# Spreading the inverse sums of an attention kernel: whole-array matmuls against row tiles of 32

## The reference

```
sc = where(causal, q k^T / 4, -inf), cut into key windows of 128
probs = e / sum(e)        with e = exp(sc - max), inside each window of 128 keys
attn  = softmax(probs)    over all 1024 keys; then attn @ v
```

## Time and profile before

| | |
|---|---|
| Three runs, median (lowest to highest) | 2868.73 us (2865.2 to 2870.33) |
| Profiled execution: span (no time of its own is given) | 2862.7 us |
| Mean granted clock of TensorE over the span | 0.967 of full speed |
| PE, DVE, ACT, POOL busy, share of the span | 90%, 76%, 63%, 21% |
| Last chain of work: PE, DVE, waiting for nothing shown, ACT | 49%, 29%, 15%, 4% |
| Of it, by line: L1152, L1075, L565, L516, L618, L580 | 11%, 7%, 7%, 6%, 5%, 3% |

### The profile page before, as it was taken

How to read it: one execution, slowest core, us unless ns; L and a number is a source line. 1 busy time by engine, 2 the same in 40 slices (tenths; PEclk the granted TensorE clock), 3 DMA queues, 4 the chain that set the end, 5 groups by cost and what they waited for, 6 DMA issues and landing times.

```text
span 2862.7 us, 58460 instructions
## 1 busy us (share of the span) xinstructions
PE 2562.9 (90%) x21797; PEld 1415.5 (49%) x21884; DVE 2179.6 (76%) x2854; ACT 1810.4 (63%) x2772; POOL 589.1 (21%) x518
## 2 busy tenths in 40 slices
PE   4799898999989999899989999899898999989877
PEld 2354464444544455444554445554464444644444
DVE  4687868788778877878778787787868888688755
ACT  2288844887358772677627886288843888358761
POOL 0012023120322104220132212212123120321004
PEclk8699999999999999999999999999999999999998
DMA  3412211231121220222202212022311131121000
GB/s 109 82 24 65 41 52 35 41 65 33 43 57 30 54 53 26 54 34 49 55 28 50 60 24 74 13 46 60 43 55 35 31 75 24 52 56 24 1 30 15
DMA packets 97791, 128.66 MB, mean 45 GB/s; under 512 B 21064, under 2 KB 58184, under 8 KB 97488
## 3 DMA queue, kind: packets, MB, share of 16 engines
q1 hardware_dynamic: 97488, 124.58, 20.4%
HBM read 90.94 MB, written 33.60 MB: 44 GB/s over the span
## 4 chain that ended last, share of the span: by engine, by line
PE 49%; DVE 29%; issue 15%; ACT 4%; POOL 1%; DMA 1%; DVEq 1%; SPq 0%; POOLq 0%; ACTq 0%
DVE e L1152 11%; DVE negmax L1075 7%; PE dd L565 7%; PE ring L516 6%; PE st L618 5%; PE st L653 3%; PE dd L728 3%; PE ring L580 3%; PE st L708 3%; DVE r_a L1188 2%; PE st L728 2%; PE dd L708 2%; DVE r_b L1185 2%; ACT e L899 2%; PE dd L461 2%
## 5 line engine op out<-in xcount | busy, mean ns | idle before, releaser
L1075 DVE TENSOR_REDUCE negmax<-ring 128x8 f32<-128x1024 f32 (+1 forms) x640 | 691.1, 1111 | 225.7 <-PE ring L519 225.3
L885 ACT ACTIVATE e<-st 128x512 f32<-128x512 f32 x1152 | 661.2, 597 | 265.3 <-PE st L621 143.3
L1152 DVE TENSOR_TENSOR e<-ring,e 128x1024 f32<-128x1024 f32 x576 | 667.3, 1217 | 76.2 <-PE ring L580 74.4
L899 ACT ACTIVATE e<-e 128x1024 f32<-128x1024 f32 x576 | 593.5, 1052 | 55.4 <-DVE e L1152 39.0
L618 PE MATMUL st<-q_st,k_st 128*128 128x256 bf16 (+3 forms) x2272 | 456.6, 278 | 13.7 <-ACT e L885 8.3
L516 PE MATMUL ring<-k_st,q_st 96*128 96x512 bf16 (+3 forms) x1536 | 397.0, 340 | 40.5 <-DVE negmax L1075 29.5
L580 PE MATMUL ring<-r_p,sel 128*128 128x256 bf16 (+3 forms) x2272 | 333.9, 273 | 73.9 <-DVE e L1152 61.7
L565 PE MATMUL dd<-e,d_ones 128*32 128x256 f32 (+2 forms) x4864 | 368.2, 379 | 0.0
L1231 POOL TENSOR_TENSOR r_a<-r_b,r_h 128x256 f32<-128x256 f32 (+1 forms) x96 | 79.8, 832 | 1253.6 <-ACT r_h L862 1253.6
L653 PE MATMUL st<-e,v 128*32 128x256 f32 (+3 forms) x4608 | 300.3, 384 | 25.9 <-ACT e L899 25.9
L618 PEld LDWEIGHTS st<-q_st,k_st 128*128 128x128 bf16 x2304 | 187.7, 98 | 239.9 <-issue 80.8
(11 more groups left out here) (137 smaller groups left out, 3120.4 us busy)
## 6 DMA issues: line engine op xcount, KB each, us to landing
q_st<-q_parts SPq DMA_DIRECT2D x192, 128.0 KB, 4.4
k_st<-k_parts SPq DMA_DIRECT2D x192, 128.0 KB, 6.8
q_parts<-qk_p SPq DMA_DIRECT2D x16, 768.0 KB, 3.5
k_parts<-qk_p SPq DMA_DIRECT2D x16, 768.0 KB, 4.2
x_in<-in_x SPq DMA_DIRECT2D x9, 1024.0 KB, 6.7
x_res<-in_x SPq DMA_DIRECT2D x8, 1024.0 KB, 6.3
e<-in_wfcT SPq DMA_DIRECT2D x8, 1024.0 KB, 5.0
e<-in_wprojT SPq DMA_DIRECT2D x16, 512.0 KB, 7.0
```

The source lines that it names most:

```text
L885: act.activation(e[:, hh, BANK * u:BANK * u + BANK], st[:, BANK * (n % 2):BANK * (n % 2) + BANK], ACT.Exp, scale=DK ** -0.5).then_inc(s["e ...
L899: act.activation(v, v, ACT.Exp).then_inc(s["e2_done"], 1)
L1075: dve.tensor_reduce(negmax[:, hh % 2, 8 * t:8 * t + w], slot[:, 0:P * w].rearrange("p (a n) -> p a n", n=P), AX_X, ALU.max, negate=True).t ...
L1152: dve.tensor_tensor(v, ring[r % 2][:, :].rearrange("p (i n) -> p i n", i=2), v, ALU.mult).then_inc(s["ring_free"], 1)
```

## The change

The loops over heads and strips are exchanged, and both operands are cut to the 32 partitions of the head. `sel` is zero on the other 96 partitions in the columns of this head, so the sum is the same. Weights of 32 x 128 are loaded, and 32 rows of `r_p` are streamed. The two heads of a slot own neighbouring strips of 32 rows and write to two different banks.

```
-                        for i in range(2):
-                            hh = 2 * pair + i
-                            for (j, qa, qb), c in columns(u):
-                                mm = pe.matmul(ring[r % 2][:, BANK * i + c:BANK * i + c + qb - qa], sel[:, NB * hh + j:NB * hh + j + 1].to_broadcast([P, P]), r_p[:, qa:qb],
-                                               start=True, stop=True, skip_group_check=True)
+                        for (j, qa, qb), c in columns(u):
+                            for i in range(2):
+                                hh = 2 * pair + i
+                                rows_hh = slice(32 * hh, 32 * hh + 32)
+                                mm = pe.matmul(ring[r % 2][:, BANK * i + c:BANK * i + c + qb - qa], sel[rows_hh, NB * hh + j:NB * hh + j + 1].to_broadcast([32, P]),
+                                               r_p[rows_hh, qa:qb], start=True, stop=True, skip_group_check=True)
                         mm.then_inc(s["ring_ready"], 1)
```

## The result

Measured in runs side by side, the changed kernel takes 2890.48 us (median of 4 runs, 2883.98 to 2894.71), the kernel before 2868.27. The ratio is 1.0073, interval 1.0058 to 1.0087: slower by 0.7%, clear of the noise. That lies outside the range, on the side of rival B, and past its 2876.7. The profiled execution has a span of 2892.1 us (before: 2862.7) and a mean granted clock of 0.929 (before: 0.967).

What follows compares the result with a forecast made beforehand. DVE was taken to bound plain spread stages, with the path through L580 in groups 0 and 1. From 2868.7 us, gains of 22.0 less 8 for six clock falls gave 2854.7, range 2842 to 2875.

Steps and rivals of the forecast that it cites:

- rival B: Spread stages: the clock falls often and stays down; twelve falls of 2.5 us cost 30, giving 2876.7 us; chance 0.16.
- One slot: L580 on PE: a slot takes 0.39 us instead of 0.61, 0.21 saved, as its two heads' matmuls run side by side.
- The drain: Where L580 meets L453 and L461 in groups 0 and 1: each change of tiling adds 0.10 us.
- group 0: Seven spread stages with transposes L453 between slots and products: gain 1.04 us each, 7.3 in all, with ACT next bound.
- group 1: Seven spread stages with projections L461 between slots and products: gain 0.82 us each, 5.7 in all.
- The sum of 22.0: All spread stages: 9.0 us from 18 plain ones, 7.3 from group 0 and 5.7 from group 1, before clock falls.
- a plain stage: Eighteen spread stages without inserted transposes or projections, bounded by DVE: gain 0.50 us each, 9.0 in all.
- The price of a fall: Spread stages at half clock: each fall costs 0.75 to 1.75 us, taken as 1.3.
- The number of falls: Clock falls at the 25 thin places (all spread stages but group 1's): bounds 0 and 25, six taken, 8 us.
- The thinnest place: Between two units' products: PE busy 2.10 us of 3.50 before, some 1.4 after, so the clock falls in some.
- Its sign, a mean clock under 0.95: Clock mean under 0.95 would prove the main case wrong and point to rival B; the main case expected about 0.96.
- Rival C: Row strips in L580 do not overlap, heads run in series; drains add 4 us, 2873, middle 2871; chance 0.11.

## Why the prediction was wrong, step by step

- **One slot: right.** 0.39 for 0.61, and 218.6 us of L581 where 220 was forecast. The step from column strips to row strips held, and the two matmuls of a pair start 3 to 4 ns apart.
- **The drain: right.** 0.10 at L453 by the rows above. The Trainium skill (TensorEngine Tiling (Array Packing), Key Properties) says that a change of the tiling mode drains the engine; the trace agrees, with those 0.10 us. The 4 us that I put on it for groups 0 and 1 don't follow from my own sum: ACT bounds group 0 there, so only group 1's 7 x 0.3, some 2 us, would come back.
- **The sum of 22.0: right.** The kernel with full clock in all its spread stages (two fillers, none in group 1) has a span of 2841.4, 21.3 below before; by medians it is 17.9. The 21.3 hold some luck, since that execution has 182 us of low clock outside the spread stages and before has 192. By terms: a plain stage wins 0.21 at its start and 20.46 - 20.07 = 0.39 inside, 0.60 (0.50 was forecast); group 0 wins 1.0 in the stage of the change that kept its clock (1.04) and 0.8 with fillers; group 1 wins 0.44 and 0.24 around it, 0.68 (0.82), for its waits shrink to 1.58 and 1.46 and not to 1.4 and 1.3. Times 18, 7 and 7 that is 21. ACT takes over in group 0 as forecast: its exponentials run back to back there.
- **The price of a fall: too small.** Against full-clock stages of 20.8, 23.3 and 20.1 us the 32 stages of the change lose some 50 us, 2.0 a fall; I had 1.3, and 1.75 at most. Per us of low clock the price is near (50 over 218 us, 0.23; the forecast had 1.3 for 5.1 us, 0.25), but low clock lasted 8.7 us a fall on average. A plain stage that fell lost 1.1 to 3.1 us, mostly over 10 to 14 us of low clock, one of group 0 mostly 1.5.
- **The number of falls: this step failed.** I wrote "the number of falls has no row; bounds 0 and 25. I take six, 8 us". It was 25: 24 of the 25 places that I named, and one stage of group 1. The thinnest place itself came out as forecast, with PE busy 1.38 us of 3.50 where I had some 1.4:

```profile
1336.40:1339.90 3.50, 1.38 (x20) 1.00 1.06 135
```

My own rows had the clock fall behind 1.71 of 3.40 and hold behind 1.84, and 1.38 is below both; six was a number without a reason. Two slots issued together even run at once, eight matmuls in 0.40, since all four heads lie on different strips. What I left out besides are the rows: I judged by PE's time alone, and the clock also fell behind 2.11 us busy of 3.40 (1337.9 to 1341.3), where before it held behind 2.00 and 1.84. The matmuls fill a quarter of the rows each; the stretch from 82 to 134 us, which I gave to rival B, pointed that way. With both steps as measured the forecast would have been 2862.7 - 22.0 + 50 = 2890.7 for the span; it is 2892.1.
- **Rival B** had mechanism and sign right, with 12 falls for 25 at 2.5 us for 2.0, and a chance of 0.16. Its sign, a mean clock under 0.95, came with 0.929. The Trainium skill (TensorE: Matmul & The Clock Gate, Why this matters for your kernels) says to avoid PE-idle gaps between bursts of matmuls above a length that no rest here reaches. By that sentence no spread stage of the change would fall, for the longest rest in them is 1.38 us (0.88 before); 25 fell, and the measurement decides. The sentence says nothing of rows, and the run with 72-row fillers shows that they count.
- **Rival C** is out: row strips overlap in every run with 32-row tiles.

What stays open: how time and rows weigh against each other, and why the low clock lasted some 26 us of a stage with 72-row fillers but 3 to 14 in the change, and where the 7 us of the kernel with tiles in groups 0 and 1 only are won. The numbers per run are chance to a degree: in the change alone the four runs spread over 10.7 us, in the kernel before over 5.1.

## What to carry to other kernels

A change that frees the matrix engine where something else is the bound buys rests, and rests can cost the clock: look at what the engine does in the thinnest stretch afterwards, not at its mean, and count the rows its matmuls fill as well as their time. Here tiles only in the groups with inserted work came to 0.9974 with no further change, though most of group 0's stages fell even so. Useless whole-array matmuls in the rests gave most of the forecast gain (17.9 of 22.0 us by medians), but check every run for the clock: fillers over 72 rows cost more than none (1.0211 against 1.0073).

## What the runs showed of the hardware that I had not expected

- Matmuls on different strips of 32 rows run as separate streams. Issued head after head, a slot took the same 0.40 us as by turns, and its pairs started 10 to 12 ns apart; two slots issued together took 0.40 for eight matmuls of 256 columns on four strips.
- The clock can fall with PE's time unchanged. Fillers of equal length over 128 and over 72 rows gave mean clocks of 0.969 and 0.940 in the profiled executions, and 2850 and 2924 us as medians. The 56 rows that make the difference hold zeros in the fillers' weights, so rows count even where their weights are zero.
- Low clock outlives an engine that is busy nearly all the time: 28.53 us of 29.40 at a mean clock of 0.56, with matmuls over 32, 72 and 128 rows mixed.
